# Whole 128-row transfers and builds, and VectorE in place of GpSimd for splitting edge attributes, in a three-layer graph convolution

## The reference

```
m = concat([h[dst], h[src], edge_attr], axis=1) @ W + b      # one row per edge
h = segment_sum(m, dst, num_segments=12500)                  # relu after layers 1 and 2
x = layernorm(x + h)                                         # after layer 3
```

## Time and profile before

| | |
|---|---|
| median of 3 runs | 2943.17 us (2933.61 to 2949.12) |
| profiled execution, its own time | 2934.42 us |
| its span, first to last instruction | 2932.6 us |
| mean granted TensorE clock | 0.981 |
| TensorE busy | 2777.2 us (95%) |
| VectorE busy | 1528.2 us (52%) |
| ScalarE busy | 1282.8 us (44%) |
| GpSimd busy | 2024.0 us (69%) |
| DMA | 489.51 MB, 167 GB/s |

### The profile page before, as it was taken

The page is one execution under the profiler, slowest core; times in us unless marked ns, Lnnn a source line. Parts: engine busy times, 40 slices in busy tenths (PEclk is TensorE's granted clock), DMA queues, the critical chain, the costliest instruction groups (busy, mean ns, idle before and its releaser), DMA issues.

```text
span 2932.6 us, 60066 instructions
## 1 busy us (share of the span) xinstructions
PE 2777.2 (95%) x23143; PEld 1772.5 (60%) x23143; DVE 1528.2 (52%) x3219; ACT 1282.8 (44%) x2335; POOL 2024.0 (69%) x2141
## 2 busy tenths in 40 slices
PE   2599999999999999999879999999998999999998
PEld 1266666666666666666546666666665666666665
DVE  7999999999999999997211111111111212121111
ACT  5698988889898898986000000000000000000000
POOL 5377676767767767676477777777727878777773
PEclk9799999999999999999889999999999999999999
DMA  4534535354453534435968989888877899988882
GB/s 95 141 108 131 145 104 168 108 152 125 118 158 102 167 109 138 138 104 171 228 156 212 219 212 215 211 215 208 212 198 175 209 211 211 214 210 211 210 209 48
DMA packets 242619, 489.51 MB, mean 167 GB/s; under 512 B 156178, under 2 KB 191708, under 8 KB 214213
## 3 DMA queue, kind: packets, MB, share of 16 engines
q1 hardware_dynamic: 136846, 272.20, 34.9%
q10 hardware_dynamic: 58404, 143.10, 18.2%
q0 software_dynamic: 47088, 70.34, 12.4%
HBM read 341.80 MB, written 143.65 MB: 166 GB/s over the span
## 4 chain that ended last, share of the span: by engine, by line
PE 85%; DVE 5%; POOL 4%; issue 3%; DMA 2%; ACT 1%; SPq 0%; ACTq 0%; POOLq 0%; DVEq 0%
PE ps L1279 37%; PE ps L1287 20%; PE ps L1259 13%; POOL far_rows L717 3%; PE ps L1355 3%; PE ps L1316 3%; PE ps L1306 2%; PE ps L1356 2%; DVE is_key L1036 2%; PE ps L1320 1%; PE ps L1341 1%; DVE is_low L1026 1%; ACT blocks L810 1%; PE ps L1330 1%; DMA dst_stage<-in_dst 1%
## 5 line engine op out<-in xcount | busy, mean ns | idle before, releaser
L717 POOL DMA_INDIRECT far_rows<-parts,far_src x1350 | 1490.0, 1104 | 511.8 <-issue 364.4
L1279 PE MATMUL ps<-blocks,parts 125*128 125x375 fp8e4 x7500 | 1550.2, 324 | 4.1 <-ACT blocks L810 2.4
L810 ACT ACTIVATE blocks<-ps 125x505 fp8e4<-125x505 f32 x1875 | 1117.1, 758 | 143.2 <-PE ps L1259 140.3
L1279 PEld LDWEIGHTS ps<-blocks,parts 125*128 125x128 bf16 x7500 | 737.7, 100 | 422.7 <-issue 18.3
L1259 PE MATMUL ps<-is_key,is_low 128*125 128x505 bf16 x1875 | 707.0, 387 | 36.4 <-DVE is_key L1036 15.4
L1036 DVE TENSOR_SCALAR is_key<-from_one,parts 128x500 bf16<-128x500 f16 x1875 | 687.5, 414 | 3.5 <-PE ps L1259 1.6
L1287 PE MATMUL ps<-blocks,parts 125*64 125x375 fp8e4 x7500 | 685.8, 326 | 0.0
L1287 PEld LDWEIGHTS ps<-blocks,parts 125*64 125x64 bf16 x7500 | 398.5, 110 | 275.1 <-issue 154.2
L1133 DVE COPY z<-ps 125x256 f32<-125x256 f32 x51 | 21.7, 425 | 895.0 <-PE ps L1356 876.6
L1259 PEld LDWEIGHTS ps<-is_key,is_low 128*125 128x125 bf16 x1875 | 257.6, 138 | 223.0 <-DVE is_key L1036 39.9
L1060 DVE SCALAR_TENSOR_TENSOR far_masks<-far_dst,from_one 128x750 fp8e4<-128x750 int32 (+1 forms) x125 | 195.3, 1562 | 308.5 <-PE ps L1320 294.1
(11 more groups left out here) (125 smaller groups left out, 1414.5 us busy)
## 6 DMA issues: line engine op xcount, KB each, us to landing
blocks<-counts SPq DMA_DIRECT2D x100, 1066.4 KB
counts<-blocks ACTq DMA_DIRECT2D x25, 4101.6 KB
blocks<-counts SPq DMA_DIRECT2D x100, 984.4 KB
far_rows<-parts,far_src POOLq DMA_INDIRECT x1350
blocks<-counts SPq DMA_DIRECT2D x100, 123.8 KB
counts<-blocks ACTq DMA_DIRECT2D x25, 476.1 KB
blocks<-counts SPq DMA_DIRECT2D x100, 114.3 KB
attr_stage<-in_edge_attr SPq DMA_DIRECT2D x125, 88.0 KB, 1.9
```

The costliest lines, as they stand in the source:

```text
L717: nc.gpsimd.indirect_dma_start(far_rows[:, g % 2, j, :], None, parts_d[layer], bass.IndirectOffsetOnAxis(ap=far_src[:, g % BATCHES, j:j + ...
L810: nc.scalar.activation(blocks[0:L, b % 2, :, n * W:(n + 1) * W], build[0:L, c % BUILD, 0:COLS].rearrange("p (t w) -> p t w", w=W), ACT.Cop ...
L1279: nc.tensor.matmul(acc_ps(g), parts[0:L, layer % 2, t, 0:2, :].rearrange("p k d -> p (k d)"), blocks[0:L, g % 2, t, :], start=(t == 0), st ...
```

## The change

1. `counts`, `rows_d`, `h_rows` and `node_rows` get 128 rows; the store and the loads of blocks, and the store and the load of node rows between layers, are one transfer of 128 rows in place of two. `is_low` is 128 x 5 x 128, the build matmul has 128 output rows, and ScalarE converts 128 rows. Input x, the output and the stores of feature parts stay as they were.
2. The four operations of the split go from GpSimd to VectorE, in its loop at n, n+1, n+2 and n+3 for n in SPLIT_AT. GpSimd's queue in layer 0 holds only the 450 gathers, one after another.
3. Near masks move to n = 5, 19, 28, 42 and 54, far masks to 9, 30 and 51.
4. One more memset at the start clears rows 96 to 127 of `node_rows`.

```diff
-    MASK_AT = [BUILDS * u // UNITS + 3 for u in SUM_AFTER[0:NEAR]]
-    FAR_MASK_AT = [18, 42, 57]
+    MASK_AT = [FIRST_MASK_AT, 19, 28, 42, 54]
+    FAR_MASK_AT = [9, 30, 51]
+    SPLIT_AT = [1, 13, 22, 36, 45, 58]
...
-    counts = nc.dram_tensor("counts", (BATCHES, L, WORDS), bf16).ap()
+    counts = nc.dram_tensor("counts", (BATCHES, P, WORDS), bf16).ap()
...
-        is_low = sb("is_low", [P, 2, LOWS, L], bf16)
+        is_low = sb("is_low", [P, 2, LOWS, P], bf16)
...
-                for r in range(2):
-                    rows = slice(ROWS[r], ROWS[r + 1])
-                    sp.dma_start(block_words[rows, g % 2, words], counts[b, rows, words]
-                                 ).then_inc(block_loaded[g % 2][q], DMA)
+                sp.dma_start(block_words[:, g % 2, words], counts[b, :, words]).then_inc(block_loaded[g % 2][q], DMA)
...
             for g in range(BATCHES):
-                for k in range(PER_BATCH):
-                    split_attr(g * PER_BATCH + k)
-                    if k < NEAR:
-                        for j in range(GATHERS[k], GATHERS[k + 1]):
-                            gather_rows(g, j)
+                for j in range(FJ):
+                    gather_rows(g, j)
+            pool.wait_ge(attr_split, GROUPS * PARTS)
...
-                act.dma_start(counts[b, rows, :], block_words[rows, b % 2, 0:WORDS]
+                act.dma_start(counts[b, :, :], block_words[:, b % 2, 0:WORDS]).then_inc(counts_stored[b % 2], DMA)
...
+            def split_high(n):
+                s = n % RING
+                dve.wait_ge(attr_landed[s], landed_of(n))
+                if n >= 2:
+                    dve.wait_ge(attr_summed, n - 1)
+                nc.vector.tensor_copy(attr_part(n, 0), attr_values(n)).then_inc(attr_split, 1)
+
+            def split_left(n):
+                dve.wait_ge(attr_split, n * PARTS + 1)
+                nc.vector.tensor_tensor(attr_values(n), attr_values(n), attr_part(n, 0), ALU.subtract).then_inc(attr_left, 1)
+
+            def split_mid(n):
+                dve.wait_ge(attr_left, n + 1)
+                nc.vector.tensor_copy(attr_part(n, 1), attr_values(n)).then_inc(attr_split, 1)
+
+            def split_low(n):
+                dve.wait_ge(attr_split, n * PARTS + 2)
+                nc.vector.tensor_tensor(attr_part(n, 2), attr_values(n), attr_part(n, 1), ALU.subtract).then_inc(attr_split, 1)
...
-                nc.tensor.matmul(build[0:L, c % BUILD, 0:COLS], is_low[:, c // LOWS % 2, c % LOWS, :],
+                nc.tensor.matmul(build[:, c % BUILD, 0:COLS], is_low[:, c // LOWS % 2, c % LOWS, :],
```

More of the change, by code:

```diff
@@ L92, in gnn_kernel @@
     S = D + ED + 1
[L94 removed]
+    rows_d = [nc.dram_tensor(f"rows_{n}", (BATCHES, P, T, D), fp32).ap() for n in range(1, LAYERS)]
     feats = [x] + [nc.dram_tensor(f"feats_{n}", (N, D), fp32).ap() for n in range(1, LAYERS)]
[L96 removed]
+    counts = nc.dram_tensor("counts", (BATCHES, P, WORDS), bf16).ap()
     parts_d = [nc.dram_tensor(f"parts_{n}", (N, PARTS * D), bf16).ap() for n in range(LAYERS)]
@@ L486, in load_h, with h_loads, node_stores @@
             if layer:
-                engine.wait_ge(nodes_stored[(g - BATCHES) % 2], ((g - BATCHES) // 2 + 1) * 2 * DMA)
-            table = rows_d[layer - 1][b, :, :, :] if layer else x[b * B:(b + 1) * B, :].rearrange("(t p) d -> p t d", p=L)
-            for r in range(2):
-                rows = slice(ROWS[r], ROWS[r + 1])
-                engine.dma_start(h_rows[rows, g % 2, :, :], table[rows, :, :]).then_inc(h_loaded[g % 2], DMA)
+                engine.wait_ge(nodes_stored[(g - BATCHES) % 2], node_stores(g - BATCHES))
+            if layer:
+                engine.dma_start(h_rows[:, g % 2, :, :], rows_d[layer - 1][b, :, :, :]).then_inc(h_loaded[g % 2], DMA)
+            else:
+                table = x[b * B:(b + 1) * B, :].rearrange("(t p) d -> p t d", p=L)
+                for r in range(2):
+                    rows = slice(ROWS[r], ROWS[r + 1])
+                    engine.dma_start(h_rows[rows, g % 2, :, :], table[rows, :, :]).then_inc(h_loaded[g % 2], DMA)
+        def h_loads(g):
+            return sum(1 if k >= BATCHES else 2 for k in range(g % 2, g + 1, 2)) * DMA
+        def node_stores(g):
+            return sum(2 if k >= LAST else 1 for k in range(g % 2, g + 1, 2)) * DMA
         def load_attr(engine, g):
@@ L512, in store_nodes @@
             layer, b = divmod(g, BATCHES)
+            engine.wait_ge(nodes_ready, g + 1)
             if layer < LAYERS - 1:
-                table = rows_d[layer][b, :, :, :]
-            else:
-                table = out[b * B:(b + 1) * B, :].rearrange("(t p) d -> p t d", p=L)
-            engine.wait_ge(nodes_ready, g + 1)
+                engine.dma_start(rows_d[layer][b, :, :, :], node_rows[:, g % 2, :, :]).then_inc(nodes_stored[g % 2], DMA)
+                return
+            table = out[b * B:(b + 1) * B, :].rearrange("(t p) d -> p t d", p=L)
             for r in range(2):
@@ L584, in load_block @@
                     sp.wait_ge(applied, g - 1)
-                    sp.wait_ge(counts_stored[g % 2], ((g - 2) // 2 + 1) * 2 * DMA)
-                sp.wait_ge(counts_stored[b % 2], (b // 2 + 1) * 2 * DMA)
-                for r in range(2):
-                    rows = slice(ROWS[r], ROWS[r + 1])
-                    sp.dma_start(block_words[rows, g % 2, words], counts[b, rows, words]
-                                 ).then_inc(block_loaded[g % 2][q], DMA)
+                    sp.wait_ge(counts_stored[g % 2], ((g - 2) // 2 + 1) * DMA)
+                sp.wait_ge(counts_stored[b % 2], (b // 2 + 1) * DMA)
+                sp.dma_start(block_words[:, g % 2, words], counts[b, :, words]).then_inc(block_loaded[g % 2][q], DMA)
             for g in range(2):
@@ L804, in keep_counts @@
                 if n == 0 and b >= 2:
-                    act.wait_ge(counts_stored[b % 2], b // 2 * 2 * DMA)
+                    act.wait_ge(counts_stored[b % 2], b // 2 * DMA)
                     act.wait_ge(applied, b - 1)
@@ L815, in store_counts @@
                 act.wait_ge(kept, (b + 1) * BUILDS)
-                for r in range(2):
-                    rows = slice(ROWS[r], ROWS[r + 1])
-                    act.dma_start(counts[b, rows, :], block_words[rows, b % 2, 0:WORDS]
-                                 ).then_inc(counts_stored[b % 2], DMA)
+                act.dma_start(counts[b, :, :], block_words[:, b % 2, 0:WORDS]).then_inc(counts_stored[b % 2], DMA)
             def scale_rows(b):
-                act.wait_ge(h_loaded[b % 2], (b // 2 + 1) * 2 * DMA)
+                act.wait_ge(h_loaded[b % 2], h_loads(b))
                 act.wait_ge(deg_kept, b + 1)
```

65 lines of the change are left out of this document (33 added, 32 removed).

## The result

The changed kernel takes 2892.91 us (median of 4 runs, 2890.71 to 2894.31); beside it the kernel before took 2939.4. The ratio is 0.9838, with a 95% interval of 0.9808 to 0.9868: 46.5 us faster. Forecast were 26.7 us and 2916 us, with a range from 2898 to 2945: the direction was right, the gain nearly twice as large, and the time outside the range.

A forecast was written before the change was run, and what follows sets the result against it. TensorE was taken to bound layer 0, with VectorE close behind. 9.7 us from steady batches and 17.0 from the passage to layer 1 made 26.7, taken from the median 2943.2 for 2916 us, range 2898 to 2945.

The forecast's parts named there:

- part 3: Transfers: one issue replaces two, 2.4% more bytes, DMA share 0.90 in layers 1 and 2; 0 in the sum.
- Part 1, the price: VectorE in layer 0: splits 5.6 us a batch, `is_low` 0.3, freed 4.3; net +1.6 against 2.7 of room, so hidden.
- The rival in which VectorE becomes the bound: Layer 0: splits at twice the price exceed VectorE's room, 3034 us, or 2996 with the upper bound alone; chance 0.12.
- Part 1, chunk 65: Layer 0: without GpSimd's interference TensorE's 0.42 us wait for a key goes in 23 batches, 9.7 us gained.
- Part 2: Builds of 128 rows: weight load falls from 137 to 100 ns but lies under the previous matmul; 0 in the sum.
- Part 4, the last batch: Last batch of layer 0: TensorE's waits for splits and far rows go, 11.5 us, and far sums run 1.3 us shorter.
- Part 4, the rest of the passage: Passage to layer 1: applies and degree turns at full clock, 4.2 us gained before GpSimd's first gather of layer 1.
- only the steady part gains: Passage: TensorE arrives sooner but finds the first block or features' store late; -12 us, 2931 us; chance 0.07.

The follow-up runs named there:

- A: Kernel before with 128-row builds, stores and loads alone, GpSimd still splitting: 2905.70 us against 2937.86, ratio 0.9886.
- build_only: Kernel before with only `is_low` and the build matmul at 128 rows, on a chip of the second kind: 3356.87 us, ratio 0.9990.
- C: Changed kernel with blocks stored and loaded in two pieces, of 112 and 16 rows: 2915.93 us, ratio 0.9920 to the kernel before.
- D: Changed kernel with blocks stored and loaded as two halves of 64 rows: 3013.84 us, ratio 1.0273 to the kernel before.
- E: Changed kernel with blocks stored and loaded as even and odd rows, 64 each: 2894.02 us, ratio 0.9850 to the kernel before.
- F: Changed kernel with VectorE's masks back at their old places: 2900.63 us, ratio 0.9882 to the kernel before.
- B: Kernel before with only the split on VectorE and the new mask places, transfers in two pieces: 2921.66 us, ratio 0.9940.
- Q: Changed kernel with TensorE waits at layer 0's chunk 65 and after convolutions in layers 1 and 2, second kind of chip: 3714.27 us, ratio 1.1022.
- P: Changed kernel with one added TensorE wait at chunk 65 of layer 0's batches, second kind of chip: 3607.84 us, ratio 1.0694.

## Why the prediction was wrong in size

**The step that failed is part 3.** It said "0 in the sum; a row for each engine of sixteen is 8 at most in both versions". I had counted rows for an engine. A shows 32 us for the transfers and builds, `build_only` nothing for the builds, C the share going back from 0.66 to 0.89 with two pieces, and D and E what the count left out: where in SBUF the rows of a piece lie. The passage, which I had seen as waiting for a store and for attributes, was the place where a quicker transfer is not hidden. The words "DMA is busy 0.88 with TensorE never idle" are true of layers 1 and 2 and say nothing of the last batch of layer 0.

**Part 1, the price.** Forecast 5.6 us a batch; by the distances above 5 x 4 x 0.25 + (0.22 + 0.50 + 0.22 + 0.37) = 6.3. Freed: keys, 75 x (416 - 349) ns = 5.0 against 4.3, and `is_low` costs nothing (822 ns against 819, not 2.4% more). The net was over-priced: VectorE is busy 906.3 of the 950 us, 48.8 us a batch, and was 884.8, 48.2 a batch. That is +0.6 and not +1.6, so GpSimd's splits had cost VectorE some 5.7 us a batch, near the upper bound of 5.9; the keys' durations show 5.0 of them. The rival in which VectorE becomes the bound did not come on chips of the first kind.

**Part 1, chunk 65.** The mechanism was right, the term too small: forecast 9.7 us, measured 13.1 (23 x 0.57; the batch before the last alone gives 1.5 of them). Without the new mask places, which the sum gave no gain, most of it would have been lost again (F).

**Part 2** was right: the weight load of a build takes 99 ns and not 137, it lay under matmuls all the same, and the ratio of the build alone is 0.999 (measured on a chip of the second kind, in whose layer 0 that kernel keeps the full clock).

```profile
L1284 PEld LDWEIGHTS ps<-is_key,is_low 128*128 128x128 bf16 x1396 | 137.2, 99 | 123.3
```

**Part 4, the last batch.** 12.8 us forecast (11.5 + 1.3), 13.95 measured. The waits vanished one by one as listed. But their cause was half told: they needed both the splits in GpSimd's queue and attributes that land late behind the block's store, and A removes them without touching the queue.

**Part 4, the rest of the passage.** 4.2 us forecast for applies at full clock, 8.8 measured to the first gather. The clock did stay at 1.00, but 4.7 of the 8.8 are the features' store, 4.37 us from issue to gather where it took 9.05. Behind that gather come 2.7 us more, and 4.1 in the rest, 3.5 of them between the end of layer 1 and the end of layer 2's third batch: this second passage was not in the sum at all.

In all: steady 14.4 with batch 0 against 9.7, last batch 13.95 against 12.8, then 15.6 against 4.2. The last is the miss, and B shows what it hung on: without the transfers, the split's 14 us in the last batch come back as 14 us in the passage, and my "only the steady part gains" would have been near the truth. That C comes out at 2915.93 us, on my forecast of 2916, is luck: against the kernel before, its last batch gains 14 us and its passage loses 13.7, which is not how the 2916 was made up.

## What to carry to other kernels

Transfer whole 128-row tiles, or, where pieces are needed, take every second row for each, the form that E shows to be as fast; check the DMA share beside the GB/s, since the same bytes at a higher share are a transfer in poor pieces. Before pricing a transfer at nothing because it is hidden in the steady part, look at the passages between stages, where the same queue carries the last store and the next stage's first loads. When two parts of a change cure the same wait, time each alone: their gains don't add by reasoning, and a gain in one place can be given back at the next transfer.

## What was not expected of the hardware

The same bytes, in as many pieces of the same size, take 10.8 us to land as halves and 5.2 us as even and odd rows (D, E). A slow store delays small loads issued behind it: attributes come 4.1 us a batch late for VectorE in D.

Chips differ in more than speed. On the second kind the kernel before takes 14% longer. In `build_only`, which takes the same time, nearly all of that lies in layers 1 and 2: a typical batch takes 37.6 us against 29.07, and in every kernel tried there it takes 36 to 39 us, with holes in TensorE's work that no semaphore explains. In layer 0 the kernels with GpSimd splitting hold 1.00 and 51.6 to 51.9 us a batch on it, and those with VectorE splitting take 61 to 64 us. Ahead of the fall to 1.2 GHz shown above TensorE had stopped for 6.35 us, after a stretch in which it was busy 9.6 to 10 of every 10 us at 2.4 GHz.

The traces point at GpSimd's gathers. These are, in the changed kernel on such a chip, the last but one batch of layer 1, the last one, and the last but one of layer 2 (columns as in the earlier trace rows):

```profile
2507.14:2542.34 35.20, 32.73 (x257) 19.18 (x256) 4.37 (x7) 2.21 (x7) 21.51 (x21) 0.95 0.57 178
2542.34:2571.42 29.08, 29.08 (x257) 18.82 (x256) 4.37 (x7) 2.22 (x7) 0.00 (x0) 1.00 0.57 191
...
3430.10:3464.70 34.60, 32.24 (x257) 19.07 (x256) 5.62 (x9) 1.41 (x3) 20.63 (x20) 0.95 0.27 72
```

The middle one has the same matmuls, four loads of blocks and the same DMA share as the first, but no gather, and it runs at the full clock in 29.08 us. The third has gathers and no load of blocks, and is slow. The last batch of each layer, in which GpSimd gathers nothing, is as fast on the second kind as on the first in all ten runs there (29.1 us in layers 1 and 2, 29.8 with Q's pauses; 35.4 in layer 0 where VectorE splits). In layer 0 the stops fall into the burst of 18 gathers too. The one shown above is near its end:

```profile
446.96 0.95 POOL L726 DMA_INDIRECT far_rows<-parts,far_src  x1 [0.30 <-issue]
```

In batches 1 to 23 of that run all 22 stops of TensorE over 2.5 us begin 19.5 to 22.6 us into the burst, which takes 26 to 27 of the 61 us. Where GpSimd splits, its gathers come three or four at a time, and batches 1 to 23 have no such stop. So the burst, which part 1 of the change brought into layer 0, is the nearest suspect. It is not shown to be the cause there: no run has VectorE split and the gathers spaced out, and on the first kind the same bursts stop nothing. The DMA share doesn't tell the windows of layer 0 apart (0.38 in both), and the added rests of P and Q did not help.

A version that takes the transfers alone is the safe one: 0.989 on the first kind and 0.973 on the second, while the whole change gives 0.984 and 1.046.
